# Attention and mixture of experts on one core: seven PSUM banks with a release semaphore each, the reciprocals of the sums spread by TensorE, and another task table

## What is computed

```
s1 = q1 k1^T / 4 + causal mask;  s2 = q2 k2^T / 4 + causal mask
out = (softmax(s1) - lam * softmax(s2)) v          # v: 32 channels per key group
out = (out - mean) * rsqrt(var + eps) * gn_w + gn_b # over tokens and channels of a head
x = layernorm(x + 0.8 * out Wo)
routed = expert_of(x)(x * sigmoid(top logit));  shared = FFN(x)      # 8 experts, top 1, F = 512
x = layernorm(x + routed + shared)
```

## Time and profile before

| | |
|---|---|
| Time, median of 3 runs | 848.89 us (846.95 to 850.22) |
| Profiled execution: its own time | 850.68 us |
| Profiled execution: its span | 848.9 us |
| TensorE, VectorE, ScalarE, GpSimd busy | 78%, 67%, 54%, 29% |

### The profile page before, as it was taken

How to read it: one execution, slowest core, us unless ns; L and a number is a source line. 1 busy time by engine, 2 the same in 40 slices (tenths; PEclk the granted TensorE clock), 3 DMA queues, 4 the chain that set the end, 5 groups by cost and what they waited for, 6 DMA issues and landing times.

```text
span 848.9 us, 13242 instructions
## 1 busy us (share of the span) xinstructions
PE 659.7 (78%) x4306; PEld 440.6 (52%) x4306; DVE 570.5 (67%) x1274; ACT 459.7 (54%) x1400; POOL 246.8 (29%) x214
## 2 busy tenths in 40 slices
PE   7476767886768788976687886777778798999993
PEld 3243334553444356534443564444345548999993
DVE  2749989989588697886886888669963341443432
ACT  2477778889437468874465678647763011111110
POOL 0053431024262310322633000101100124666653
PEclk9777798997776999967679998678889889999998
DMA  3695039200003933000049072001000037877630
GB/s 129 154 327 151 26 70 217 39 1 0 1 26 77 184 56 64 1 0 1 26 100 179 14 194 67 1 1 39 19 1 1 25 104 240 269 256 259 250 122 1
DMA packets 54500, 78.33 MB, mean 92 GB/s; under 512 B 10231, under 2 KB 41725, under 8 KB 52608
## 3 DMA queue, kind: packets, MB, share of 16 engines
q1 hardware_dynamic: 45728, 64.50, 28.5%
q10 hardware_dynamic: 4880, 6.16, 2.6%
q0 software_dynamic: 3824, 6.83, 2.5%
HBM read 58.06 MB, written 22.15 MB: 94 GB/s over the span
## 4 chain that ended last, share of the span: by engine, by line
PE 44%; DVE 28%; ACT 15%; issue 6%; POOL 3%; DMA 2%; ACTq 1%; SPq 0%; POOLq 0%; DVEq 0%
ACT w_exp L1142 10%; PE wide_ps L1030 10%; DVE mneg L1364 9%; DVE w_exp L1387 6%; PE pv_ps L845 4%; PE wide_ps L807 3%; PE wide_ps L878 3%; PE wide_ps L780 3%; PE misc L925 2%; DVE diff L1387 2%; PE misc L1041 2%; PE pv_ps L1041 2%; PE misc L789 2%; PE s_ps L829 2%; PE misc L953 2%
## 5 line engine op out<-in xcount | busy, mean ns | idle before, releaser
L1142 ACT ACTIVATE w_exp<-wide_ps,mneg 128x256 f32<-128x256 f32 (+3 forms) x512 | 266.9, 554 | 164.4 <-DVE mneg L1364 163.4
L1364 DVE TENSOR_REDUCE mneg<-wide_ps 128x1 f32<-128x384 f32 (+3 forms) x352 | 208.8, 633 | 42.7 <-PE wide_ps L809 41.7
L807 PE MATMUL wide_ps<-w_exp 96*128 96x256 bf16 (+3 forms) x512 | 136.8, 343 | 37.1 <-ACT w_exp L1142 28.7
L1387 DVE SCALAR_TENSOR_TENSOR w_exp<-w_exp,ratio 128x128 f32<-128x128 f32 (+3 forms) x172 | 119.3, 719 | 2.1
L1142 ACT ACTIVATION_READ_ACCUMULATOR w_exp<-wide_ps,mneg 128x1 f32 x512 | 117.2, 229 | 0.0
L807 PEld LDWEIGHTS wide_ps<-w_exp 96*128 96x128 bf16 x512 | 50.4, 110 | 103.5 <-ACT w_exp L1142 49.2
L809 PE MATMUL wide_ps<-mask,identb 128*128 128x128 bf16 (+2 forms) x352 | 96.2, 273 | 0.0
L845 PE MATMUL pv_ps<-w_exp,work 128*32 128x128 f32 (+2 forms) x532 | 63.6, 356 | 34.7 <-ACT work L1154 19.7
L1030 PE MATMUL wide_ps<-tables,w_exp 128*128 128x128 f32 x736 | 87.6, 278 | 0.0
L1030 PEld LDWEIGHTS wide_ps<-tables,w_exp 128*128 128x128 f32 x736 | 85.7, 195 | 0.1
L829 PE MATMUL s_ps<-ident,w_exp 128*128 128x128 f32 x429 | 77.5, 306 | 5.7 <-DVE w_exp L1387 3.5
(11 more groups left out here) (166 smaller groups left out, 1155.7 us busy)
## 6 DMA issues: line engine op xcount, KB each, us to landing
w_exp<-w_up_in SPq DMA_DIRECT2D x23, 1024.0 KB, 5.3
w_exp<-q_parts SPq DMA_DIRECT2D x96, 128.0 KB, 5.8
slot_tokens<-x ACTq DMA_DIRECT2D x1, 4864.0 KB, 31.9
work<-x_in SPq DMA_DIRECT2D x8, 512.0 KB, 8.1
w_exp<-w_down_in SPq DMA_DIRECT2D x8, 512.0 KB, 8.7
q_parts<-w_exp SPq DMA_DIRECT2D x6, 512.0 KB, 6.7
w_exp<-k_parts SPq DMA_DIRECT2D x18, 128.0 KB
gated_rows<-work SPq DMA_DIRECT2D x4, 512.0 KB, 6.4
```

Source lines behind the costliest of these rows:

```text
L807: nc.tensor.matmul(o[:, n], q_stack[0:KROWS, qt, (2 * g + s) * 4 + r + n, :], k_stack[0:KROWS, b % 2, 2 * g + s, 0:qt + 1, :], start=(n == ...
L1142: ins = nc.scalar.activation(probs[:, K % NPROB, s, n * w:(n + 1) * w], ring(v)[:, n * w:(n + 1) * w], ACT.Exp, bias=mneg[:, (2 * K + s) % ...
L1364: nc.vector.tensor_reduce(out=mneg[:, (2 * K + s) % 6, 0:heads], in_=ring(v)[:, 0:heads * w].rearrange("p (r k) -> p r k", r=heads), axis= ...
L1387: ins = nc.vector.scalar_tensor_tensor(diffs[K % NDIFF][:, here], probs[:, K % NPROB, 1, here], ratio[:, pair, K % 2, n:n + 1], probs[:, K ...
```

## The change

PSUM is now one tensor banks_ps of seven banks beside pv_ps. Each bank has its own semaphore, freed0 to freed6. Banks 0 to 3 serve in turn the scores and the start; banks 4 to 6 serve in turn everything else in the order in which TensorE uses them: turned differences, prep, and all tasks. A use waits only for the release of the use before it in its own bank. GpSimd no longer takes part in denom: TensorE multiplies each of 16 columns of 1/sum, read 32 times, with the identity. ScalarE takes the turned difference before the exponentials of a step, not after them. VectorE inverts the sums between the two maxima. centre is split from mean and stat is cut in four. The task table, TAIL and the steps at which GpSimd rotates and ScalarE casts are new.

```diff
-DVE_STEP = ("max0", "max1", "sums", "diff", "out", "tasks")
-ACT_STEP = ("first", "second", "lagging", "tasks")
+DVE_STEP = ("max0", "invert", "max1", "ratio", "diff", "out", "tasks")
+ACT_STEP = ("lagging", "first", "second", "tasks")
...
-put(MIDDLE, 18, "end", ("retake", 1, 1), ("project", 3, 1), ("x2", 2, 1), ("stat", 0, 0))
+put(MIDDLE, 18, "end", ("stat", 0, 0), ("retake", 1, 1), ("x2", 2, 1))
+put(MIDDLE, 19, "mid", ("project", 3, 1), ("stat", 1, 0))
...
-RING = 4
+SCORE_SLOTS, OTHER_SLOTS = (0, 1, 2, 3), (4, 5, 6)
...
+for _use in USES:
+    _kind = "score" if _use[0] in SCORE_KINDS else "other"
+    _slots = SCORE_SLOTS if _kind == "score" else OTHER_SLOTS
+    _slot = _slots[_at[_kind] % len(_slots)]
+    _at[_kind] += 1
+    _taken[_slot] += 1
+    SLOT_OF[_use], TURN_OF[_use] = _slot, _taken[_slot]
...
+        def await_freed(engine, *use):
+
+            engine.wait_ge(freed[SLOT_OF[use]], TURN_OF[use])
+
+        def take_slot(engine, *use):
+
+            if TURN_OF[use] > 1:
+                engine.wait_ge(freed[SLOT_OF[use]], TURN_OF[use] - 1)
+            return bank_of(*use)
...
-                if K >= 2:
-                    pe.wait_ge(diff_taken, K - 1)
+                here = take_slot(pe, "turn", K, 0)
...
-                    pe.wait_ge(diff_taken, KV * (J + 1))
+                    await_freed(pe, "turn", KV * (J + 1) - 1, 0)
...
-                here = far
-                v = other.next()
-                if v > 1:
-                    pe.wait_ge(far_done, v - 1)
...
-                    pe.wait_ge(denom_wide, b * QT + arg + 1)
+                    pe.wait_ge(denom_ready, b * QT + arg + 1)
                     for r in range(4):
-                        last = nc.tensor.transpose(here[:, r * P:(r + 1) * P], denomT[:, r * P:(r + 1) * P], ident[:])
+                        for g in range(KV):
+                            last = nc.tensor.matmul(here[g * DV:(g + 1) * DV, r * P:(r + 1) * P], inv1[:, arg % 2, g, r:r + 1].to_broadcast([P, DV]), ident[:],
+                                                    start=True, stop=True)
...
-            def compare(K):
+            def invert(K):
...
-                dve.wait_ge(ring_done, bank_at(b, k + 1, 1))
+                await_freed(dve, "bank", b, 2 * k + 3)
```

More of the change, by code:

```diff
@@ L126 @@
[L126 to L135, removed]
@@ L136 @@
-put(MIDDLE, 36, "end", ("shared_down", 0, 1))
-put(MIDDLE, 38, "end", ("shared_down", 1, 1))
-put(MIDDLE, 40, "end", ("shared_down", 2, 1))
+put(MIDDLE, 22, "end", ("logits", 2, 1))
+put(MIDDLE, 23, "mid", ("retake", 3, 1))
+put(MIDDLE, 24, "end", ("logits", 3, 1))
+put(MIDDLE, 25, "end", ("top", 0, 1))
+put(MIDDLE, 26, "mid", ("choose", 0, 1))
+put(MIDDLE, 27, "mid", ("rank", 0, 1))
+put(MIDDLE, 27, "end", ("ids", 0, 1))
+put(MIDDLE, 28, "mid", ("ids", 1, 1), ("ids", 2, 1))
+put(MIDDLE, 28, "end", ("shared_gate", 0, 1), ("gate", 0, 1), ("ids", 3, 1), ("shared_up", 0, 1))
@@ new lines @@
+    ("project", 3), ("logits", 1), ("x2", 2), ("retake", 2), ("x2", 3), ("logits", 2), ("retake", 3), ("logits", 3), ("top", 0), ("choose", 0),
+    ("rank", 0), ("last_gate", 0), ("last_up", 0), ("ids", 0), ("ids", 1), ("ids", 2), ("gate", 0), ("ids", 3), ("last_hid", 0), ("last_gate",
+    1), ("tables", 0), ("last_up", 1), ("tables", 1), ("last_hid", 1), ("last_gate", 2), ("last_up", 2), ("last_hid", 2), ("last_gate", 3),
+    ("last_up", 3), ("last_hid", 3), ("last_down", 0), ("last_down", 1), ("last_down", 2), ("last_down", 3))]
@@ L193, with task_uses @@
 ID_GROUPS = ((0, 1), (1, 2), (2, 4), (4, 8), (8, 13), (13, NROUTE))
-RING = 4
-RING_USES = [("start", 0, k) for k in range(8)] + [("prep", 0, arg) for name, arg, _ in HEAD if name == "prep"]
+SCORE_KINDS = ("bank", "start")
+BANK_TASKS = MISC_TASKS + ("late_gate", "late_up", "late_down", "last_gate", "last_up", "last_down")
+SCORE_SLOTS, OTHER_SLOTS = (0, 1, 2, 3), (4, 5, 6)
+NSLOT = len(SCORE_SLOTS) + len(OTHER_SLOTS)
+def task_uses(name, arg, b):
+    if name == "prep":
+        return [("prep", b, arg)]
+    if name == "drain" and NALL + arg - LAG_TURN < NALL:
+        return [("turn", NALL + arg - LAG_TURN, 0)]
+    return [(name, b, arg)] if name in BANK_TASKS else []
+USES = [("start", 0, k) for k in range(8)]
+for _name, _arg, _ in HEAD:
+    USES += task_uses(_name, _arg, 0)
 for _b in range(B):
@@ L779, in prep @@
                     for c in range(DC):
-                        last = nc.tensor.matmul(slot, wqk_sb[:, c, pair, half, :], xT[:, c, :], start=(c == 0), stop=(c == DC - 1))
+                        last = nc.tensor.matmul(here, wqk_sb[:, c, pair, half, :], xT[:, c, :], start=(c == 0), stop=(c == DC - 1))
                 last.then_inc(ring_full, 1)
@@ L998, in _ @@
                 finish_part()
-            pe.wait_ge(far_done, other.n)
-            pe.wait_ge(late_added, 2 * QT)
+            for i in range(NSLOT):
+                pe.wait_ge(freed[i], SLOT_USES[i])
             pe.wait_ge(owners_done, 1)
@@ L1407, in step @@
                         maximum(K, 1)
-                    elif piece == "sums" and 0 <= late < NALL and late % 2 == 0:
+                    elif piece == "invert" and 0 <= late < NALL and late % 2 == 0:
+                        invert(late)
+                    elif piece == "ratio" and 0 <= late < NALL and late % 2 == 0:
                         compare(late)
```

321 lines of the change are left out of this document (166 added, 155 removed).

## The result

| | changed kernel | kernel before, same chip |
|---|---|---|
| median | 801.17 us (796.03 to 802.81, 4 runs) | 848.64 us (846.95 to 850.22, 4 runs) |
| ratio | 0.9431, 95% interval 0.9384 to 0.9477 | |
| busy, profiled execution | TensorE 80%, VectorE 71%, ScalarE 58%, GpSimd 29% | 78, 67, 54, 29% |

The change makes the kernel 47 us faster. The prediction said 806, with a range of 782 to 838. The profiled execution has a span of 801.0 us, against 848.9.

The account below looks back on a forecast made before the run. VectorE's waits in the batches were taken to bound the kernel. Gains of 15 + 23 + 14 + 2 + 4 = 58 us, less 15, left 43: 850.7 to 807.7 profiled, 806 us median, range 782 to 838.

Parts of the forecast that it names:

- What bounds the kernel: VectorE leads in the four batches and loses time waiting for other engines; the experts are TensorE's and stay untouched.
- The copy's order: ScalarE copies the turned difference before the exponentials: TensorE's 51.8 us wait nearly vanishes, 15 us of VectorE's score waits return.
- Projections and FFN: VectorE's waits for output projections (31.1 us) and shared FFN (29.1 us) shrink, giving back 23 and 14 us.
- Denom at nothing: Reciprocal task on TensorE: 16 matmuls replace four transposes at no cost, 0.65 us against 0.63 us.
- the bound of 30: Reciprocal tasks: if the 16 matmuls didn't run side by side, 16 tasks would put 30 us on TensorE.
- Reciprocals between the maxima: VectorE inverts the sums between the two maxima: 2 us of a 5.4 us wait for ScalarE return, no loss.
- The tail: After the batches, the rank goes ahead of a gate product, the tables ahead of a hidden-layer product: 4 us gained.
- The haircut: A quarter, 15 us, off the 58 us sum, since VectorE reaches its next waits sooner; leaves 43 us.
- half gain: Rival: waits in the batches move instead of going; 15 to 25 us gained, 825 to 838 us, chance 0.20.
- GpSimd unpaced: Rival: without reciprocal copies, GpSimd's rotations slow VectorE's subtractions by 5 to 10 us, 811 to 816; no separate chance.
- Slower: Rival: ScalarE waits for transposes before its exponentials, from about 88 of 176 steps; 10 to 45 us slower, chance 0.07.
- The named checks: Signs to confirm the forecast: TensorE's weighing waits, batch times, VectorE's projection and FFN waits, reciprocal task length, experts' TensorE time.

Follow-up runs that it names:

- the ladder: Kernels on one chip from the kernel before, 847.9 us: copy's order 828.3; denom on TensorE, VectorE's order, cut tasks, bank semaphores 815.2; new banks 784.2; new table 799.6.

## Why the prediction came out right

**What bounds the kernel** held. The gain lies in VectorE's waits in the batches, and the experts did not move.

**The copy's order** was right in mechanism and too small: 15 us predicted, 19 to 24 measured. The count of score waits was near: put back in the changed kernel, the old order makes VectorE wait 16.5 us more for score banks (38.4 for 21.9) and 2 more for projections; the new order in the kernel before takes 9.1 and 1.7 off, and 7.8 at the shared FFN (29.1 to 21.3). The prediction gave the copy a share in the projections' 23 us, and of that there is little.

**Projections and FFN** were 23 + 14 = 37 us for the copy, the banks and the denoms together. The waits fell by 19.6 and 17.0 us, 36.6 in all. The banks alone measured 31 us and more as time. So as waits the sum of these terms holds; most of it is the bank plan, which the prediction put only beside the copy and the denoms. With the old bank plan all the other edits together gain only 1.1% over the kernel before, which the text did not foresee.

**Denom at nothing** was the step that failed in the detail. The row of 16 was read as 16 products. In the changed kernel 16 products are 32 records and take 1.08 us; the row was eight products. So the sentence that the trace's 0.65 us agrees with the page rests on half a task. 16 tasks x (1.08 - 0.63) = 7 us more on TensorE, an estimate at full clock, inside the bound of 30; TensorE's idle time was to cover it, which no run tests. What the edit brought, 14 to 18 us, was booked in other terms.

The chain of the changed kernel's tail has the two kinds of product side by side, 32 records with 32 weight columns and 8 with all 128:

```profile
591.94 1.01 PE banks_ps L949 x32
592.95 3.63 PE banks_ps L924 x8
```

A record of L924 covers 512 columns in 0.45 us, or 128 in 0.11; a record of L949 covers 128 in 0.032, 3.6 times faster. The Trainium skill (TensorEngine Tiling (Array Packing), section Tiling Modes (Key Properties)) has different tiles work independently and in parallel; with four column tiles of 32 the trace agrees.

**Reciprocals between the maxima**: 2 us predicted, 5 to 9 measured, and the expected fall of the wait was wrong (5.4 to 17.2).

**The tail**: 4 us predicted, 75 to 71 measured in the windows.

**The haircut** of 15 us was given the wrong reason. It was to stand for waits that move on. The terms sum to 58; the ladder gives 20 + 13 + 31 = 64 without the table. What brings it to 47 or 48 is the new table, 14 to 17 us the wrong way, and the prediction had no term for a loss by the table's places at all. Two errors of about one size met, 43 us net where the other edits gave 64, and nothing for a table that costs 14 to 17. That was luck, and not precision, and it put 806 next to 801.

**The rivals.** The half gain's mechanism, differences coupled to tasks by banks in strict order, is there (10.0 us at L875 for L1510, and the chain at 263 us) without its size. GpSimd unpaced: the sign came true, with 17 subtractions over 2 us for 13 before and 10.4 us more for all of them (187.3 for 176.9). The mechanism did not. With the old table GpSimd's copies are gone too, and subtractions and ratios together take 208.4 us, for 208.5 before; with the copies back in the changed kernel they take 218.0, for 215.6. So the longer subtractions come with the new table, and the old rotation steps alone do not help. The Trainium skill (GPSIMD Engine Reference, section 1 Specifications) says that the SBUF interfaces are shared with VectorE; the 5.02 us for two subtractions beside 2.35 + 2.53 us of GpSimd agree. Slower: its sign came true as well, ScalarE does wait for transposes, 57.5 us, and taking 36 us of that away gave 0.4%. A sign of this kind, without a size, could not tell the rival from the forecast.

**The named checks**: weighing under 10, measured 1.5; batches 150, 150 and 122, measured 153, 155 and 124; projection about 8, measured 11.5; FFN about 15, measured 12.1; reciprocal task 0.6 to 0.7, measured 1.08; experts 129, measured 128.7.

What stays open: of the table's 14 to 17 us, some 6 are likely the first projection's place. By the trace the FFN stretch of the two middle batches loses 10 (19.2 and 19.7 us for 14.4 twice), of which the steps just before give some back (24 to 27 take 8.8 us for 11.2), and the last batch loses 4.5 (120.2 for 115.7, from its first maximum to that of its last step). No kernel that moves only those rows was run.

## What to carry to other kernels

When one PSUM bank serves unlike tasks, count the uses of it that wait for a release by another engine; three banks in turn for them, with four kept for the scores, were worth 31 us here, more than any other edit. A change made of several edits has to be run with each edit taken out: the new table came in the same change as the banks and is a loss with either bank plan, 1.7% on the new one. A wait's size tells little by itself: 7 us more at the reciprocals came with VectorE's new order and a gain of 5 to 9, 36 us less at the copies brought 4 to 5.

## What was not expected of the hardware

A product with float32 operands appears as two matmul records (a transpose as one), so 32 records stand for 16 products and 1.08 us. And VectorE's smallest two-input instruction is held as long as a large one: with the rotation steps moved, a ratio of 128x4 elements took 2.12 us where it takes 0.21. GpSimd's rotation started 0.25 us ahead of it, and both end at 186.5:

```profile
184.12 2.36 POOL L562 TENSOR_TENSOR work<-w_exp,tables 128x1024 f32<-128x1024 f32 x1 [3.59 <-ACT w_exp L1105]
184.37 2.12 DVE L1421 SCALAR_TENSOR_TENSOR ratio<-total,neglam,inv 128x4 f32<-128x4 f32 x1
```

It isn't peculiar to that run: a ratio of 128x8 took 2.11 us in the changed kernel (170.62) and one of 128x2 took 2.04 in the kernel before (595.68), each beside a GpSimd instruction of 2.35 us. In these rows what counts is how long the GpSimd instruction on SBUF still runs, not how much VectorE has to move.
